# The last token-choice layer in two parts of 1024 tokens, the first begun before the last chunk is routed

## The reference, cut to what matters

```
# _L3_xcond_ref
score = einsum('nqh,hk,nlk->nql', decoder_h_t, W_a, encoder_outputs), masked to a window
context = einsum('nql,nlh->nqh', softmax(score) * gauss, encoder_outputs)
x = x + tanh(concat([context, decoder_h_t]) @ W_c.T)
...
# _L3_ffn_ref
router_probs = softmax(xt @ Wr + br); gates = max(router_probs); idx = argmax(router_probs)
xn = (xt - mu) * rsqrt(var + 1e-5) * ln_g + ln_b
h = relu(einsum('te,td,edf->tf', one_hot(idx, 8), xn, W1) + b1[idx])      # 128 -> 512
y = (einsum('te,tf,efd->td', one_hot(idx, 8), h, W2) + b2[idx]) * gates   # 512 -> 128
x = x + y
```

## Time and profile before

| | |
|---|---|
| median of 3 runs | 918.86 us (916.9 to 919.8) |
| span of the profiled execution, first to last instruction | 904.5 us |
| what lies between the two | 14.4 us |
| busy: PE / DVE / ACT / POOL | 709.5 / 471.9 / 243.3 / 248.6 us |
| last token-choice layer: first `up` to last `down` on PE | 818.2 to 873.3 us |
| from there to the end of the span | 31.2 us |

### The profile page before, as it was taken

The page is one execution under the profiler, slowest core; times in us unless marked ns, Lnnn a source line. Parts: engine busy times, 40 slices in busy tenths (PEclk is TensorE's granted clock), DMA queues, the critical chain, the costliest instruction groups (busy, mean ns, idle before and its releaser), DMA issues.

```text
span 904.5 us, 13708 instructions
## 1 busy us (share of the span) xinstructions
PE 709.5 (78%) x4589; PEld 453.8 (50%) x4589; DVE 471.9 (52%) x1390; ACT 243.3 (27%) x377; POOL 248.6 (27%) x326
## 2 busy tenths in 40 slices
PE   4567999999999899784599838689877967529960
PEld 3553445444444545453499814244442757518950
DVE  6547785747656555567322135354337357663432
ACT  1112323232223333231144402123223722103310
POOL 4821010010204121535200064611130037860014
PEclk9657999999999999886799966689899996558995
DMA  9910000000001300001122110100000050002112
GB/s 360 417 52 1 0 1 1 0 1 0 1 0 33 155 2 1 24 19 35 59 71 72 51 38 21 34 2 1 1 1 1 2 186 1 19 31 64 43 42 84
DMA packets 25350, 43.58 MB, mean 48 GB/s; under 512 B 3265, under 2 KB 19393, under 8 KB 24130
## 3 DMA queue, kind: packets, MB, share of 16 engines
q1 hardware_dynamic: 22210, 36.41, 11.2%
q0 software_dynamic: 3072, 6.30, 2.4%
HBM read 26.05 MB, written 16.65 MB: 47 GB/s over the span
## 4 chain that ended last, share of the span: by engine, by line
PE 66%; DVE 15%; POOL 7%; issue 4%; DMA 3%; ACT 2%; SPq 1%; DVEq 0%; POOLq 0%; ACTq 0%
PE banks L338 62%; POOL SHARE L2113 2%; DVE mx L1400 2%; DVE stats L983 2%; PE banks L345 2%; DMA SHARE<-rows_out,slots 2%; POOL XN L2002 1%; POOL rstd L1995 1%; PE banks L768 1%; ACT XNT L1701 1%; POOL rows_in L2129 1%; DVE mv L988 1%; POOL SELECT L2057 1%; PE banks L895 1%; DVE X L999 1%
## 5 line engine op out<-in xcount | busy, mean ns | idle before, releaser
L1995 POOL TENSOR_TENSOR rstd<-veps,neghalf 128x4 f32<-128x4 f32 x32 | 33.1, 1035 | 390.9 <-DVE veps L991 390.8
L338 PE MATMUL banks<-XNT,SLOT 128*128 128x512 f32 x256 | 124.8, 611 | 4.1 <-DVE cw L1261 4.1
L338 PE MATMUL banks<-U 128*128 128x128 f32 (+3 forms) x816 | 123.2, 387 | 1.8 <-ACT U L1868 0.9
L2113 POOL DMA_INDIRECT SHARE<-rows_out,slots x48 | 46.0, 958 | 165.3 <-DMA rows_out<-SHARE 151.7
L1762 ACT ACTIVATE SHARE<-banks,SM 128x512 f32<-128x512 f32 x68 | 46.7, 687 | 154.0 <-PE banks L338 153.9
L338 PEld LDWEIGHTS banks<-U 128*128 128x128 f32 (+3 forms) x816 | 82.4, 182 | 10.5 <-issue 7.7
L1400 DVE TENSOR_REDUCE mx<-banks 128x8 f32<-128x616 f32 x64 | 51.2, 800 | 66.7 <-PE banks L338 65.6
L1284 DVE SCALAR_TENSOR_TENSOR SHARE<-banks,SM,SHARE 128x512 f32<-128x512 f32 x68 | 51.0, 750 | 62.9 <-PE banks L338 59.7
L338 PEld LDWEIGHTS banks<-XNT,SLOT 128*128 128x128 f32 x256 | 50.0, 196 | 67.5 <-issue 67.2
L1802 ACT ACTIVATE U<-banks 103x1536 f32<-103x1536 f32 x32 | 46.4, 1450 | 81.7 <-PE banks L338 81.7
L338 PE MATMUL banks<-SHARE,SLOT 128*128 128x512 f32 x128 | 66.9, 603 | 0.0
(11 more groups left out here) (298 smaller groups left out, 1157.5 us busy)
## 6 DMA issues: line engine op xcount, KB each, us to landing
rows_in<-U SPq DMA_DIRECT2D x1, 8192.0 KB, 33.4
SLOT<-l1w SPq DMA_DIRECT2D x2, 2048.0 KB, 22.2
SLOT<-f SPq DMA_DIRECT2D x2, 2048.0 KB, 10.1
U<-rows_in SPq DMA_DIRECT2D x64, 64.0 KB, 1.8
SLOT<-l3w SPq DMA_DIRECT2D x2, 2048.0 KB, 8.5
rows_out<-SHARE SPq DMA_DIRECT2D x14, 256.0 KB, 2.3
SLOT<-w SPq DMA_DIRECT2D x1, 2048.0 KB, 13.5
SM<-small SPq DMA_DIRECT2D x1, 1376.5 KB, 9.1
```

What stands on the lines that cost most here:

```text
L338: return nc.tensor.matmul(out_, lhsT, rhs, start=start, stop=stop, **kw)
L1995: power = g.tensor_tensor(rstd[:, a, :], veps[:, a, :], neghalf[:], ALU.pow)
L2113: g.indirect_dma_start(YG[:, j % RING, :], None, ys[0:BLOCKS[l] * P, :], bass.IndirectOffsetOnAxis(ap=slots[:, t, k:k + 1].bitcast(u32), a ...
```

## The change

Layer 7's tokens are taken as two parts: part 0 is chunks 0 and 1, part 1 is chunks 2 and 3. Each part has its own regions in HBM (`rows_in`, `rows_in2`), its own count, list of blocks and result tensor. 1024 tokens need at most 8 + 7 = 15 blocks, so 2 x 15 = 30 blocks are done, in groups of 4, 4, 4, 3 and again 4, 4, 4, 3. Layer 3 stays one part of 39 blocks.

- `place(0)` and `place_tokens(0)` run on DVE right behind `finish(1)`, inside the attention's loop. That loop is one round shorter: the routing of chunk 3 moves into `topk_layer`, on DVE between the relus of blocks 0, 1 and 2.
- `place(1)` is cut into six steps ahead of the relus of blocks 3 to 8, `place_tokens(1)` stands ahead of that of block 9.
- PE waits for the scatter of chunk 1 only, does `busy` and `rows_in(0)`, and then chunk 3's transposition and logits ahead of `up(0)`.
- SP issues the loads of group g+3 behind the store of group g (from g = 1), where it was g+4.
- POOL gathers chunks 0 and 1 when part 0's four groups are stored; DVE combines these eight tiles behind the relus of blocks 20 to 27. The other eight are gathered at the end.
- A second zeroing DMA of 4 MB follows the first, and one small DVE instruction is added to `constants`.

```diff
-BLOCKS = {l: NT * k + E1 - 1 for l, k in CHOICES.items()}
+PART_BLOCKS = {1: NT * 2 + E1 - 1, 3: NT // 2 + E1 - 1}
+PARTS = {1: 1, 3: 2}
+BLOCKS = {l: PARTS[l] * n for l, n in PART_BLOCKS.items()}
...
+COUNT_AT, PLACE_FROM, PLACE_STEPS, COMBINE_FROM = 3, 3, 6, 20
...
 # PE, topk_layer
-                pe.wait_ge(sem(f"scattered{s}_{BATCH - 1}"), 16 * TPC * CHOICES[l])
+                pe.wait_ge(sem(f"scattered{s}_{BATCH // PARTS[l] - 1}"), 16 * TPC * CHOICES[l])
                 busy(BUSY_LOAD)
                 rows_in(0)
+                if l == 3:
+                    prep_xt(4 * s + BATCH - 1)
+                    logits(BATCH - 1)
                 for b in range(BLOCKS[l] + 2):
...
+                    if l == 3 and b == COUNT_AT:
+                        count(BATCH - 1)
...
 # DVE, window_layer
-                for i in range(BATCH + (2 if ahead else 1)):
+                for i in range(BATCH + 1):
...
                         finish(c)
+                        if c == 1:
+                            for step in range(PLACE_STEPS):
+                                place(0, step)
+                            place_tokens(0)
...
 # DVE, topk_layer
+                relu(0)
+                route(last)
+                for step in range(4):
+                    choose(last, step)
+                relu(1)
+                choose(last, 4)
+                relu(2)
+                finish(last)
+                for b in range(3, BLOCKS[l]):
+                    if PLACE_FROM <= b < PLACE_FROM + PLACE_STEPS:
+                        place(1, b - PLACE_FROM)
+                    if b == PLACE_FROM + PLACE_STEPS:
+                        place_tokens(1)
+                    relu(b)
+                    if COMBINE_FROM <= b < COMBINE_FROM + 2 * TPC:
+                        c, k = divmod(b - COMBINE_FROM, TPC)
+                        combine(s, l, c, k)
...
 # POOL
-                    if s == len(layers) - 1:
-                        for c in range(BATCH):
-                            gather(s, l, c)
+                    for p in range(PARTS[l]):
+                        stored = GROUPS_OF_BLOCKS[l] * (p + 1) // PARTS[l]
+                        pool.wait_ge(sem(f"slots_ready{s}"), CHOICES[l] * (p + 1))
...
+                        if s == len(layers) - 1:
+                            for c in range(p * BATCH // PARTS[l], (p + 1) * BATCH // PARTS[l]):
+                                gather(s, l, c)
...
 # SP, move_rows
+                late = 1 if PARTS[l] > 1 else 0
+                for g in range(4):
                     load(g)
-                for g in range(n_groups):
+                for g, (first, n) in enumerate(groups):
                     drained(sp, ("Yd", s, g))
...
-                    if g + 4 < n_groups:
-                        load(g + 4)
+                    if g >= late and g + 4 - late < len(groups):
+                        load(g + 4 - late)
```

More of the change, by code:

```diff
@@ L326, in scaled_rows, with place_of, inner_downs, rows_count @@
             return sem(f"ln_scaled{n // BATCH}"), TPC * (n % BATCH + 1)
+        def place_of(l, b):
+            g = max(g for g, (first, _) in enumerate(BLOCK_GROUPS[l]) if first <= b)
+            first, n = BLOCK_GROUPS[l][g]
+            return g, b - first, b - first == n - 1
+        def inner_downs(l, b):
+            return done_before[l] + sum(not place_of(l, n)[2] for n in range(b + 1))
+        def rows_count(l, g):
+            return 16 * sum(n for i, (_, n) in enumerate(BLOCK_GROUPS[l]) if i <= g and i % 4 == g % 4)
         def group_of(c, k):
@@ L438, in window_layer @@
                 front(1)
-                for i in range(1, BATCH + (3 if ahead else 1)):
+                for i in range(1, BATCH + 1):
                     c = i - 2
@@ L1601, in topk_layer @@
                         heads_prep(key)
-                place_tokens()
-                for b in range(BLOCKS[l]):
-                    if l == 1:
-                        if b >= UP_RING:
-                            up_weight(b)
-                    else:
-                        relu(b)
+                    place_tokens(0)
+                    for b in range(UP_RING, BLOCKS[l]):
+                        up_weight(b)
+                    return
+                norms, route, choose, finish = routing(s, 3)
+                last = BATCH - 1
+                relu(0)
[15 more added lines that the diff above has]
+                        combine(s, l, c, k)
             def choice_layer(s):
@@ L1684, in _ @@
             if layers[-1][0] == TOPK:
-                for c in range(BATCH):
+                for c in range(BATCH // 2, BATCH):
                     combine(len(layers) - 1, layers[-1][1], c)
@@ L1729, in window_layer @@
                 exps(0)
-                for i in range(1, BATCH + (2 if ahead else 1)):
+                for i in range(1, BATCH + 1):
                     c = i - 2
```

251 lines of the change are left out of this document (151 added, 100 removed).

## The result

The changed kernel takes 927.1 us in the median of 20 runs (916.91 to 952.28), the kernel before 919.39 in the median of its 20. These medians of all runs lie 7.7 us apart. Some executions of either kernel run one to three per cent slower at a lower granted clock, and with these left out on both sides the ratio is 1.0116, 95% interval 1.0072 to 1.0159: 10.7 us, from 6.6 to 14.6. The forecast was 3.8 us faster, its range ended at 922.5.

What follows compares the result with a forecast made beforehand. PE bounds the block stretch, with chunk routing before and gathers after it; -12.6 + 16.2 + 0.6 + 0.3 + 1.5 - 10.0 + 0.2 = -3.8 us, from 918.86 to 915.1 us, range 911 to 922.5.

Steps and rivals of the forecast that it cites:

- The lead: Last layer up to the first block: earlier placing and chunk work, plus earlier clock rise, save 12.6 us (11.3 to 13.2).
- Seven more blocks: Block loop on PE: seven added blocks at 2.315 us each cost 16.2 us, the largest and surest term.
- DVE among the blocks: First blocks: DVE's relus, routing and placing make PE wait 0.6 us before down(3), then DVE keeps up; bounds 0 and 3.
- The clock: PE's granted clock rises earlier, so fewer first blocks run at 1.2 GHz: 1.3 us gained, between 0 and 1.9.
- Loads: SP's loads with one group less of lead: PE waits 1.5 us, at group 5 only; bounds 0 and 4.
- The rival of late loads: SP bounds the loop's second half; groups 4 to 7 wait 9.0 us instead of 1.5; time 922.6; chance 0.13.
- Eight gathers less at the end: After PE's end eight gathers remain instead of sixteen, saving 10.0 us; bounds 9.5 to 10.1.
- The rival by which gathers wait for relus: Early gathers each wait for two relu blocks, 3.5 us apart; PE loses 4.9 us; time 920.0; chance 0.05.
- The others hide: Part 0's eight gathers, landing from block 19 on, one per 1.25 us, stay hidden beside the blocks.
- 14.4 us around the span: Time outside the profiled span, added to the forecast span of 900.7 us to give 915.1 us.

Runs made afterwards that it cites:

- the three edits: Changed kernel with the register read ahead, all combines behind the block loop, loads of groups 4 and 5 both behind group 1's store: ratio 1.025.
- `PLACE_FROM` 5: Kernel with register ahead, combines at end, groups 4 and 5 loaded together, gathers paced, its second-part placing begun one more block later: ratio 1.001 to before.

## Why the prediction was wrong, by its own steps

- **The lead, 12.6 us (11.3 to up(0), 1.3 by the clock behind it).** Right, and a little short. Placing with slots took 801.61 to 807.56, 6.0 (forecast 6.1). Up(0) stands 62.8 us behind the layer's start, 13.3 nearer than before, where 11.3 (64.8) was forecast: chunk 3's transposition and logits ran at full clock, 0.66 and 1.06 us where the prediction had 1.09 and 1.87. Of the gain behind up(0) about half came, 0.6 us by the granted clock. The absolute 806 to 808 missed, because layer 6 began 16 us later by chance.
- **Seven more blocks, 16.2 us.** Right as PE's work: with the causes below removed, the loop is 21.0 us longer than before, of which these are 16.2.
- **DVE among the blocks, 0.6 us, "so it keeps up".** This is the step that failed. The block was priced by its four instructions, 1.15 us, and costs 2.08 with its register's load. Rectification 3 was done 13.0 us behind the end of up(0), not 10.5, and down(3) waited 1.72 us, not 0.6; behind it rectifications were 2.5 to 3.4 us apart as long as placing went on (834.23 to 851.86: six intervals in 17.6 us, forecast 2.3 each), and 2.5 apart with the combines between them. In the loop the fixes for DVE (register ahead, combines at the end, placing later) and for the loads brought 83.2 down to 73.4 (83.3 to 73.4 on one chip), so **9.8 of the 12.9 missing microseconds** lie there. The loads' part of them is 2.1 to 3.7 us, the rest DVE's by difference. A third of the 9.8 (0.93 against 0.97 on average, 5.3 against 1.9 us lost) was half clock behind waits.
- **The clock.** The prediction gave it one term, the gain of 1.3 us at the start, and priced every wait at its own length. In the runs a wait of 1.1 us (group 5's load) cost 3.7 where half clock followed and 2.1 where none did. Waits of 0.4 to 1.6 us ahead of group 4, in the seven runs with the three edits, had none behind them, so a price of several times its length is not a rule.
- **Loads, 1.5 us.** Right in place (group 5 alone) and length (1.14), wrong in price, as just said. The rival of late loads at groups 4, 6 and 7 did not occur in the changed kernel.
- **Eight gathers less at the end, -10.0 us.** Right: 9.9. The rival by which gathers wait for relus is refuted: 0.94 us each, 1.25 apart, beside them. The Trainium skill (SBUF — State Buffer, "A bandwidth-pool intuition that's wrong (but worth ruling out)") was cited for it with about 3100 ns beside a DVE copy; no run here shows that for indirect gathers beside these rectifications.
- **"The others hide."** True on chip 6 and in the first profile. On chips 0 and 1 the early gathers stop PE, 5 us more of the layers (174.5 to 168.8 and 169.4) and over half of what they save. The prediction looked at DVE for the victim of the gathers; it was PE.
- **14.4 us around the span.** Wrong: 1.8. The difference from the median was that execution's luck upstream. It did no harm to the difference that was forecast, but it should not have been read as a constant.

Left open: what the stop is. The profile puts no semaphore to it. In the traces of chips 0 and 1 the landings of gathers are not recorded either, where those of chips 6 and 9 and the two first profiles have them (2.5 us in the median); whether that hangs together with the stop, and whether the stop is there when no profile is taken, no run shows. Open too are the 3.1 us of the 12.9 that no edit removed. Of the loop's 21.0 us that remain over before, 4.8 are not blocks: chunk 3's routing among the first groups (group 2 to 3 is still 12.1 us against 9.3) with the half clock there, and a wait of 0.8 us for group 4's load. That these can go was not tried beyond `PLACE_FROM` 5.

## What to carry to other kernels

Price an engine's share of a pipelined block by the distance between two of its blocks when it is not waiting, not by the sum of its busy rows: a register load and what stands around it came here to 0.95 us beside 1.13 us of instructions, and an idle time that repeats to the hundredth is such a fixed cost, whoever the row blames for it. If work is to be tucked into a loop whose two engines are some 10% apart, put it where the engine that takes it has a real gap, and do not price a wait of TensorE by its length alone: 1.1 us became 3.7 where the clock fell behind it and 2.1 where it did not. And compare profiles from a common event near the change, since here 16 to 32 us came from the clock in code that nobody touched.

## What was unexpected about the hardware

- A register load on a busy DVE shows within 0.78 to 0.96 us of idle between two pieces of work, some 0.6 us of it; put behind the instructions of the block before, it is hidden (0.15 us of idle, and blocks 1.79 us apart, bound by PE).
- Eight indirect gathers 1.25 us apart slow PE in all eight profiles on chips 0 and 1, and in none of the three others, to one matmul in about 0.7 or 1.4 us for 4 us, although PE neither reads nor waits for them; spread to one per block (2.05 us apart in the mean) they do nothing. That is worth 5 us between chips of the same kind.
- TensorE's granted clock fell to its lower level in the changed kernel 1 to 2 us behind pairs of short waits (0.28 to 0.66 us) in an otherwise busy stretch, about 1.7 us lost each time; at the same pair of waits in another run (0.28 and 0.31 us) it stayed up. Idle matmuls kept it at 0.98 on average, but cost 4 us net.
